# Attention with 8-wide heads: a ring of three bank pairs, and a batch's scores in one block of four strips

## The reference

```python
q = _heads(query @ Wq.T + bq)          # 16 heads, 8 wide
k = _heads(key @ Wk.T + bk)
v = _heads(value @ Wv.T + bv)
scores = jnp.einsum('bhqd,bhkd->bhqk', q, k) / np.sqrt(D_HEAD)
scores = jnp.where(local[None, None, :, :], scores, -jnp.inf)   # layer 2: a mask from the inputs
attn = jax.nn.softmax(scores, axis=-1)
ctx = jnp.einsum('bhqk,bhkd->bhqd', attn, v)
ctx = ctx.transpose(0, 2, 1, 3).reshape(B, S, D_MODEL)
x = x + ctx @ Wo.T + bo
```

## Time and profile before

| | |
|---|---|
| median of 3 runs | 2033.67 us (2032.84 to 2035.79) |
| profiled execution, span from first to last instruction | 2027.5 us |
| what lies around the span, to the median | 6.2 us |
| busy share PE / DVE / ACT / POOL | 87% / 54% / 44% / 32% |
| mean granted TensorE clock | 0.918 of full speed |
| first stage, first to last exponential | 39.95 to 279.39 us |
| second stage, the same | 945.03 to 1202.37 us |

### The profile page before, as it was taken

The page is one execution under the profiler, slowest core; times in us unless marked ns, Lnnn a source line. Parts: engine busy times, 40 slices in busy tenths (PEclk is TensorE's granted clock), DMA queues, the critical chain, the costliest instruction groups (busy, mean ns, idle before and its releaser), DMA issues.

```text
span 2027.5 us, 48497 instructions
## 1 busy us (share of the span) xinstructions
PE 1766.7 (87%) x18886; PEld 1258.1 (62%) x18886; DVE 1092.1 (54%) x3147; ACT 891.5 (44%) x2432; POOL 652.9 (32%) x656
## 2 busy tenths in 40 slices
PE   6999985587869999998999971999699999999978
PEld 3565564576648778873565551999456666666753
DVE  4666657567532222214566763656465656665548
ACT  2333320476334444432333320666265555556525
POOL 3233201467311111103214426455133233333405
PEclk8999996788679999997999995999799999999969
DMA  5000000000000000007210001222200000000001
GB/s 174 7 13 8 2 2 9 28 16 1 1 6 1 1 2 2 1 1 293 104 76 18 18 18 45 61 57 58 90 17 17 17 17 17 6 1 1 1 1 42
DMA packets 48828, 63.55 MB, mean 31 GB/s; under 512 B 8106, under 2 KB 37701, under 8 KB 48349
## 3 DMA queue, kind: packets, MB, share of 16 engines
q1 hardware_dynamic: 44253, 51.98, 7.8%
q0 software_dynamic: 4352, 8.47, 1.3%
HBM read 32.29 MB, written 28.65 MB: 30 GB/s over the span
## 4 chain that ended last, share of the span: by engine, by line
PE 57%; DVE 9%; issue 7%; POOL 4%; POOLq 3%; DVEq 2%; ACT 1%; DMA 1%; SPq 1%; PEldq 0%; PEld 0%; ACTq 0%
PE single L1835 5%; PE quad L1823 5%; PE pair L570 3%; PE single L621 3%; PE single L2156 3%; PE quad L2139 2%; PE quad L2145 2%; PE pair L1796 2%; PE quad L598 2%; PE pair L2519 2%; POOL tokens_by_expert L417 2%; DVE arena L768 1%; PE quad L2554 1%; PE quad L2545 1%; PE single L2531 1%
## 5 line engine op out<-in xcount | busy, mean ns | idle before, releaser
L768 DVE TENSOR_REDUCE arena<-pair 128x8 f32<-128x1024 f32 x128 | 156.7, 1224 | 140.4 <-PE pair L570 138.4
L2757 POOL TENSOR_TENSOR arena<-arena 128x512 f32<-128x512 f32 x128 | 130.4, 1040 | 296.2 <-DVE arena L2676 296.2
L263 POOL TENSOR_TENSOR rstd<-var_eps,neg_half 128x4 f32<-128x4 f32 (+1 forms) x64 | 65.5, 1024 | 350.3 <-DVE var_eps L259 266.7
L748 ACT ACTIVATE arena<-quad 128x1024 f32<-128x1024 f32 x128 | 124.1, 1021 | 69.3 <-PE quad L604 65.0
L1908 ACT ACTIVATE arena<-quad,arena 128x256 f32<-128x256 f32 x256 | 110.7, 475 | 98.1 <-PE quad L1823 98.1
L892 POOL TENSOR_SCALAR arena<-arena 128x512 f32<-128x512 f32 x56 | 86.7, 1565 | 196.6 <-ACT arena L690 196.5
L570 PE MATMUL pair<-arena 32*128 32x512 f32 x512 | 147.3, 652 | 0.0
L1999 DVE TENSOR_TENSOR arena<-single,arena 128x512 f32<-128x512 f32 x32 | 22.1, 692 | 206.2 <-PE single L1835 206.2
L2612 ACT ACTIVATE arena<-pair,arena 128x128 f32<-128x128 f32 x256 | 90.9, 381 | 89.0 <-DVE arena L2671 89.0
L2612 ACT ACTIVATE arena<-quad,arena 128x128 f32<-128x128 f32 x256 | 90.9, 381 | 86.4 <-DVE arena L2671 86.4
L1835 PE MATMUL single<-wide,arena 128*64 128x128 f32 x2048 | 123.9, 275 | 0.0
(11 more groups left out here) (502 smaller groups left out, 4376.7 us busy)
## 6 DMA issues: line engine op xcount, KB each, us to landing
tokens_by_expert<-arena SPq DMA_DIRECT2D x22, 780.0 KB, 8.6
arena<-in_ctxT SPq DMA_DIRECT2D x32, 256.0 KB, 3.0
arena<-tokens_by_expert SPq DMA_DIRECT2D x72, 65.0 KB, 1.8
wide<-in_w SPq DMA_DIRECT2D x2, 2048.0 KB, 10.1
arena<-outputs_by_choice SPq DMA_DIRECT2D x16, 256.0 KB, 4.1
wide<-in_wgu SPq DMA_DIRECT2D x1, 2736.0 KB
x<-in_x SPq DMA_DIRECT2D x4, 512.0 KB, 7.9
out_x<-x SPq DMA_DIRECT2D x8, 256.0 KB, 2.3
```

What stands on the lines that cost most here:

```text
L748: act.activation(probs[n % 2][:, 8 * p:8 * p + 8, :].rearrange("p h q -> p (h q)"), T[:, 1024 * p:1024 * p + 1024], ACT.Exp).then_inc(s["s ...
L768: dve.tensor_reduce(mx[m % 2][:, 8 * p:8 * p + 8], S[:].rearrange("p (h k) -> p h k", h=8), AX.X, ALU.max).then_inc(s["s_free"], 1)
L2757: pool.tensor_tensor(part, part, inv[t % 3][:, 4 * r:4 * r + 4].unsqueeze(2).broadcast_to([P, 4, P]), ALU.mult).then_inc(s["norm_ready"], 1)
```

## The change

The six score banks form a ring of three pairs, `fours`: `pair`, the first half of `quad` and the second. Batch m has two neighbouring pairs of the ring (`halves(m)`), pairs m mod 3 and (m + 1) mod 3, for its scores and again for its turned scores. `scores(m)` writes all four banks in one block and adds once to `s_ready`; DVE's two maxima wait for this one signal. TensorE's order becomes: `turned(n)`, `scores(n+2)`, `attend(n-1)`, the turned maximum, the job. The masks stand directly ahead of the matmuls that add to them. The turned maximum moves from bank `O` to bank `M`, and a written list (`m_order`, `m_take`) says after whose evacuation each user of `M` may write. The projections of v and the output change their slots by one batch, and the rows' transposes (`turn`, `turn_rows`) stand between `turned(n)` and `scores(n+2)`. ACT's evacuations follow in the new order; DVE takes both maxima behind `normalise(n-1)`, and `moments` in the slot of `residual`.

```diff
+            fours = [pair[:, 0:1024], quad[:, 0:1024], quad[:, 1024:2048]]
+            def halves(m):
+                return fours[m % 3], fours[(m + 1) % 3]
+            def bank_of(m, r):
+                return halves(m)[r // 2][:, 512 * (r % 2):512 * (r % 2) + 512]
...
+            def m_take(pe, key):
+                if key in m_before:
+                    kind, i = m_before[key]
+                    pe.wait_ge(m_emptied[kind], i + 1)
+                return M
...
+                def scores(m):
+                    g, j = divmod(m, G)
+                    if j == 0:
+                        pe.wait_ge(s["q_evac"], g + 1)
+                        pe.wait_ge(s["kv_ready"], g + 1)
+                    if m >= 1:
+                        pe.wait_ge(s["s_free"], 2 * m)
+                    mask_banks(pe, [bank_of(m, 0), bank_of(m, 1)], mask_bias[l]["S"])
...
+                        pe.wait_ge(s["st_free"], 2 * (m - 2) + 1)
+                    mask_banks(pe, [bank_of(m, 2), bank_of(m, 3)], mask_bias[l]["S"])
+                    for r in range(4):
+                        mm = pe.matmul(bank_of(m, r), qT[g % 2][strip(r), j * P:(j + 1) * P],
...
+                    mm.then_inc(s["s_ready"], 1)
...
                 def turned(n):
+                        pe.wait_ge(s["st_free"], 2 * n)
+                    mask_banks(pe, [bank_of(n, 0), bank_of(n, 1)], mask_bias[l]["T"])
+                    pe.wait_ge(s["s_free"], min(2 * n + 3, 2 * N))
+                    mask_banks(pe, [bank_of(n, 2), bank_of(n, 3)], mask_bias[l]["T"])
...
                 for n in range(N):
                     g, j = divmod(n, G)
+                    turned(n)
+                    if j == 3 and g + 2 < NG:
+                        turn(g + 2)
                     if j == 0 and routes(g):
                         turn_rows(g - 2)
-                    mask_turned(n)
                     if n + 2 < N:
-                        mask_scores(n + 2, 0)
+                        scores(n + 2)
+                    if n >= 1:
+                        attend(n - 1)
                     if n + 1 < N:
                         turn_max(n + 1)
-                    turned(n)
-                    if n + 2 < N:
-                        scores(n + 2, 0)
-                    if n >= 1:
-                        attend(n - 1)
+                    if j == 0 and g + 1 < NG:
+                        project_q(g + 1, m_take(pe, ("q", g + 1)))
...
# DVE
-                    if n + 2 < N:
-                        maximum(n + 2, 0)
                     if n >= 1:
                         normalise(n - 1)
                     if n + 2 < N:
-                        maximum(n + 2, 1)
+                        for p in range(2):
+                            maximum(n + 2, p)
                         split_max(n + 2)
```

More of the change, by code:

```diff
@@ L461, in strip, with m_order @@
                 return slice(32 * r, 32 * r + 32)
+            def halves(m):
+                return fours[m % 3], fours[(m + 1) % 3]
+            def bank_of(m, r):
+                return halves(m)[r // 2][:, 512 * (r % 2):512 * (r % 2) + 512]
+            def m_order():
+                yield "turn", 0
+                yield "turn", 1
+                yield "mt", 0
+                for n in range(N):
+                    g, j = divmod(n, G)
+                    if j == 3 and g + 2 < NG:
+                        yield "turn", g + 2
+                    if j == 0 and routes(g):
+                        yield "rows", g - 2
+                    if n + 1 < N:
+                        yield "mt", n + 1
+                    if j == 0 and g + 1 < NG:
+                        yield "q", g + 1
+                    if j == 1 and g >= 1:
+                        yield "out", g - 1
+                    if j == 2 and g + 1 < NG:
+                        yield "v", g + 1
+                    if j == 3 and g + 2 < NG:
+                        yield "k", g + 2
+                yield "out", NG - 1
+            m_emptied = {"turn": s["xnT_ready"], "mt": s["mts_ready"], "q": s["q_evac"], "v": s["v_evac"],
+                         "k": s["k_evac"], "out": s["x_done"]}
+            if l == 2:
+                m_emptied["rows"] = s["rt_copied"]
+            m_list = list(m_order())
+            m_before = dict(zip(m_list[1:], m_list))
+            def m_take(pe, key):
[3 more added lines that the diff above has]
+                return M
             def load_ctx(sp, g):
@@ L548, in output @@
                 def output(g):
[L550 removed]
                     pe.wait_ge(s["o_free"], G * g + G)
[L552 to L553 removed]
+                    dst = m_take(pe, ("out", g))
                     for j in range(G):
[L555 removed]
+                        mm = pe.matmul(dst[:, j * P:(j + 1) * P], attnT[g % 2][:, j, :], wo[:], start=True, stop=True)
                     mm.then_inc(s["o_ready"], 1)
[L558 to L563 removed]
+                def scores(m):
                     g, j = divmod(m, G)
[L565 removed]
+                    if j == 0:
                         pe.wait_ge(s["q_evac"], g + 1)
                         pe.wait_ge(s["kv_ready"], g + 1)
[L568 to L571 removed]
+                    if m >= 1:
+                        pe.wait_ge(s["s_free"], 2 * m)
+                    mask_banks(pe, [bank_of(m, 0), bank_of(m, 1)], mask_bias[l]["S"])
+                    if m == 0:
+                        pe.wait_ge(s["k_evac"], 2)
+                    elif m == 1:
+                        pe.wait_ge(s["v_evac"], 1)
+                    else:
+                        pe.wait_ge(s["st_free"], 2 * (m - 2) + 1)
+                    mask_banks(pe, [bank_of(m, 2), bank_of(m, 3)], mask_bias[l]["S"])
+                    for r in range(4):
+                        mm = pe.matmul(bank_of(m, r), qT[g % 2][strip(r), j * P:(j + 1) * P],
+                                       kv[g % 2][strip(r), j, :, :].rearrange("p a k -> p (a k)"),
                                        start=False, stop=True, skip_group_check=True)
@@ L603, in turned @@
                         for r in range(4):
-                            mm = pe.matmul(T[:, r * 512 + a * P:r * 512 + (a + 1) * P], chooser[strip(r), a, :],
+                            mm = pe.matmul(bank_of(n, r)[:, a * P:(a + 1) * P], chooser[strip(r), a, :],
                                            mts[n % 2][strip(r), :], start=False, stop=True, skip_group_check=True)
@@ L646, in tensor @@
                 for m in range(2):
-                    for p in range(2):
-                        mask_scores(m, p)
-                        scores(m, p)
+                    scores(m)
                 pe.wait_ge(s["cvec_ready"], 1)
@@ L748, in scalar @@
                         act.activation(probs[n % 2][:, 8 * p:8 * p + 8, :].rearrange("p h q -> p (h q)"),
-                                       T[:, 1024 * p:1024 * p + 1024], ACT.Exp).then_inc(s["st_free"], 1)
+                                       halves(n)[p], ACT.Exp).then_inc(s["st_free"], 1)
+                        if p == 0 and j == 3 and g + 2 < NG:
+                            evac_turn(g + 2)
+                        if p == 0 and j == 0 and routes(g):
+                            evac_rows(g - 2)
+                    if n + 1 < N:
+                        turned_max(n + 1)
+                    if j == 0 and g + 1 < NG:
+                        evac_q(g + 1, M[:])
+                    if j == 2 and g + 1 < NG:
+                        evac_v(g + 1, M[:])
                     if j == 3 and g + 2 < NG:
```

96 lines of the change are left out of this document (21 added, 75 removed).

## The result

| | before | after |
|---|---|---|
| median time, us | 2033.26 | 2079.6 |
| profiled execution, span, us | 2027.5 | 2073.2 |
| mean granted TensorE clock | 0.918 | 0.916 |
| from the second to the last exponential, first stage, us | 232.34 | 265.78 |
| the same, second stage, us | 250.91 | 274.89 |

The changed kernel is slower: ratio 1.0225, 95% interval 1.0205 to 1.0245. The forecast was 2087.0, with a range of 2055 to 2130. The median of 2079.6 is that of four runs, one of which, at 5636 us, was disturbed; the ratio is taken without it, from runs of 2074.8 to 2080.4 us (median 2078.8). On another chip the same kernel came to 1.0176 (1.0139 to 1.0212); the experiments come back to that difference.

The account below looks back on a forecast made before the run. The prediction took TensorE to bound both stages. It added +26.7 (first stage), +18.9 (second) and +8 (clock) to +53.6; with the span of 2027.5 and 6.2 around it, 2087.3, stated as 2087 us, range 2055 to 2130.

Parts of the forecast that it names:

- The steps of the ring: Eight waits in a loop through TensorE, DVE and ScalarE, one batch per turn: 9.0 us per batch, against 7.89 before.
- Step 2: On DVE, from the reciprocal through the product to the first maximum: 1.38 us, read as 145.62 to 147.00.
- TensorE paces both: Claim that TensorE set the time of both stages before the change, busy 230.4 of 239.4 and 244.5 of 257.3 us.
- TensorE goes on setting the pace: Faster rival: a turn is TensorE's work, 6.9 us, if DVE's first maximum precedes the value products' end; about 1962 us, 4%.
- The rings: Steady turns of both changed stages: 29 intervals of 9.0 us in the first, with 265.0 us also taken for the second.
- The starts: Start of each changed stage, up to the second exponential: shorter by 6.0 us each, bounds 3 and 8.
- The clock: TensorE falling to half clock in turns without a job or with logits: seven falls at 1.2 us, +8, bounds 0 and 40.
- The routing extras of the second stage: Logits six times, 7.1 us, and counts three times, 1.5 us, now lengthening the second stage's turns.
- 53.6: Forecast total loss in us: 26.7 for the first stage, 18.9 for the second, 8 for falls of TensorE's clock.
- Four strips not at once: Rival: the four-strip score matmuls on TensorE do not run concurrently, +1.0 us x 60, about 2147 us; 5%.
- A clock that falls for long: Rival: TensorE at half clock for a third of 60 turns, 4.6 us a turn, +92, about 2171 us; 9%.
- A ring that overlaps more than it adds up: Rival: the loop's steps, measured between loaded engines, partly overlap, so half of the loss, some 2058 us; 7%.

Follow-up runs that it names:

- the filler: Changed kernel plus four transposes on TensorE, read by nobody, behind the value products of batches without a job: 2069.53 us, ratio 1.0175 to the kernel before.

## Why the prediction was right, and what in it was wrong

**The steps of the ring** (forecast, then read from the turn shown above; the turned scores began at 151.30):

| step | forecast | measured |
|---|---|---|
| 1 value products to reciprocal | 2.03 | 2.02 |
| 2 reciprocal to maximum | 1.38 | 1.24 |
| 3 first maximum and hop | 1.30 | 1.27 |
| 4 mask | 0.34 | 0.34 |
| 5 turned scores to exponential | 1.44 | 1.44 |
| 6 exponential and hop | 1.09 | 1.07 |
| 7 mask | 0.34 | 0.34 |
| 8 four-strip scores | 1.06 | 1.07 |
| sum | 8.98 | 8.79 |

The mechanism of the changed kernel is right, and doubling two of its links, on DVE and on ScalarE, lengthened the turn by 1.02 and 1.09 us. Step 2 was mis-sized: the 147.00 in the earlier trace rows isn't where the product let the maximum go. The second pass of scores, from 145.82, ended at 146.95, so that maximum was waiting for TensorE. A step read between two starts holds whatever wait stood there. The rounding of 8.98 to 9.0 did the rest.

**"TensorE paces both" was wrong.** The turns of the kernel before show it: a ring through DVE's second maximum held them, at 7.59 us with a job of 1.1 us and without one. I read the busy share of 96% and the mean interval of 7.89, where the single intervals (7.59 three times, then 8.78) would have asked for a closer look. The 7.8 us in the earlier trace rows are waits of weight loads, beside matmuls that still ran; the row of 10.3 us for L582, a wait in every turn, was in the same view and I left it out. It cost little here, since the new ring is longer. But the rival "TensorE goes on setting the pace" rested on it. Its condition, that DVE reach the first maximum before the value products end, is what the version with the maxima first brings about (maxima from 145.19, value products from 145.05 to 147.01), and the turn was 8.02 to 8.12 us there, not 6.9: TensorE still waited for the first exponential ahead of the scores, 10.9 us in 17 waits from 100 to 240 us. That price had left the exponential out. What came near it, 7.05 to 7.64, is the version with the value products first.

**The terms**, as differences to the trace before:
- *The rings.* 29 turns in each stage at 8.80 instead of 9.0: 11.6 less.
- *The starts.* 6.0 each was too little. From the first scores to the second exponential it took 25.1 us before and 16.0 after in the first stage, and 25.2 and 15.4 in the second; in the first it also began 2.2 us earlier (19.73 against 21.95). Together 21.0 instead of 12.0. The forecast had the turned scores at half clock. The clock had come back by then: the second block of scores at 24.39 took 2.09 us, but the turned scores at 28.17 ran at the upper level, and the mean clock from 19.70 to 35.75 was 0.89, where the corresponding stretch before (21.95 to 47.05) had 0.73. In the other profile of the changed kernel the turned scores, at 28.38, did run at half clock, and the second exponential came 3.2 us later, at 38.91. So some 3 us of this term are chance.
- *The clock.* Forecast +8. The long intervals, less 8.80, give 2.24 + 3.70 in the first stage and 1.12 + 2.41 + 2.28 in the second: 11.8. They stand where the forecast looked for them, at turns without a job or right behind one. Five intervals, not seven, and more for each. TensorE waited in the turns from 100 to 260 us 0.7 us for ScalarE and 0.6 for DVE on average, and from 60 to 270 us its clock was 1.00, with 82% busy. By this the rule of the Trainium skill that the prediction weighed ("TensorE: Matmul & The Clock Gate", "A second HAM failure mode: psum-queue depth-cycling") didn't decide this kernel's time; the two kernels with a doubled link come nearer to it, with falls in every third to fifth turn. The prediction's own measure was off here: the 7.8 us in 160 of the stage before were waits of weight loads, and its matmuls waited only 2.3 us for L768 and 1.9 for L778.
- *The routing extras of the second stage.* Forecast 8.6; the intervals of 9.2 to 10.2 us give 7.5. Its last interval is 6.40 against 3.98, 2.4 longer (forecast 2.2).
- *Unchanged stages.* +8.8, for which the sum had no term. 6.7 of them also lie between the two profiles of the changed kernel, so most of it says nothing about the change; the rest isn't settled.

So 53.6 - 11.6 - 9.0 + 3.8 - 1.1 + 0.2 + 8.8 = 44.7; the 9.16 and 9.15 among the first stage's intervals add 0.7, against 45.7 between the spans. The forecast of 2087 was only 7 us off because terms of either sign nearly cancelled. That is luck: the two largest errors, 11.6 and 9.0 us too slow, met 8.8 us that the sum didn't have.

**The rivals.** Four strips not at once: refuted by the 1.14 us for the four matmuls of a block. A clock that falls for long: not in the changed kernel, but with a microsecond more in each turn it came, in every third to fifth turn. A ring that overlaps more than it adds up: no, it added up within 0.2 us.

## What to carry to other kernels

An engine at 96% busy need not be the one that sets the pace. Look at the single intervals of the loop. Where turns with and without a job take the same time, look for a ring through the other engines. When a change gives buffers a new order, write down the ring from start to start, and ask for each link what stands ahead of it in its own engine's queue. Here the new layout gained 3% once the value products went first, and cost 2% with the scores first. How much of the 3% is the freed pass and how much the new order no run separates. Before a bank is asked for sooner, count who else has to be through with it.

## What the runs showed of the hardware that was not expected

- The clock and the busy time don't go together simply. From 276 to 290 us TensorE was busy in the changed kernel for 9.74 us at a clock of 0.72, and with the filler, on the same chip, for 9.97 at 1.00, though half clock itself lengthens what it does.
- Work added to a ring cost more than itself: with 1.02 and 1.09 us more of DVE and ScalarE in each turn, intervals of 11.2 to 11.5 us appeared in the steady part, some 1.4 to 1.6 above the others of the same run, with the clock at 0.85 over them. The lengthened gaps are the likely cause; no run varied them alone.
- A stage with unchanged code took 302.0 or 306.2 us in executions of the same kernel on two chips, at the same mean clock of 0.71.
- Four strips of scores took 1.14 us, two 1.08 to 1.13: the second pair of strips came almost for nothing.
